# Both passages around an attention stage reordered: the next stage's first steps issued in the stage before

## The chip, the cores and the metric

The kernel runs on one core of a Trainium2 chip as one program. The metric is device time in microseconds, the median of several runs. The engines, as the profile names them: PE is TensorE's matmul (PEld its weight load), DVE is VectorE, ACT is ScalarE, POOL is GpSimd, and SP is SyncE, which issues the DMAs. Each engine runs its own queue in order, and they wait for each other by semaphores.

## The reference

One transformer layer of "macaron" form on x of shape (8, 512, 128), in fp32: half an FFN, attention, half an FFN.

```python
x = x + 0.5 * ffn(layernorm(x))
x = x + attn(layernorm(x))
x = x + 0.5 * ffn(layernorm(x))

# ffn: 8 experts of hidden size 176, all computed, the two best weighted
scores = softmax(xf @ w_router.T)
expert_weights, expert_indices = top_k(scores, 2)
h = silu(xf @ w1[e]) * (xf @ w3[e]);  y = h @ w2[e]
out = sum over the two chosen experts of weight * y

# attn: 16 heads of complex dimension 64, causal, distance-decayed
q, k, v = x @ Wq, x @ Wk, x @ Wv          # complex
qr, kr = q * phase, k * phase             # rotation by position
E = exp(clip(-mu * |t - t'|, -30, 0))
s = Re(qr . conj(kr));  V = a * (1 - E*E) + b
maha = max(|q|^2 + E*E*|k|^2 - 2*E*s, 0) / V
logits = coef * log1p(maha / nu) - 32 * log(V);  A = softmax(causal logits)
y = concat(Re(A v), Im(A v)) @ Wo
```

## The kernel before

`program` calls three stages one after the other: `dense_phase(0)`, `attention_phase`, `dense_phase(1)`. Each is a Block of its own: all engines finish a stage before any begins the next. Matmuls in the FFN and the projections are split in three (`mm3`, lines 71 to 73: high x low, low x high, high x high), so each operand exists as a high and a low part; ScalarE makes the high part by a copy and VectorE or GpSimd the low part by a subtraction.

**The FFN.** Tokens come in 8 batches of 512, a hidden layer of 8 x 176 units in 11 chunks of 128; a slot `e` (0 to 87) is one chunk of one batch. In a slot TensorE makes `products(e + 2)` (6 matmuls of 512 columns) and `down(e - 1)` (3), ScalarE `do_silu` (L406) and the high part of hid (L511), VectorE `gate` (L714, silu times up) and `weigh` (L722, times the router's weight), GpSimd the low part `hid_lo` (L593). Layernorm, transposition and routing of later batches are put in by tables of slots (`TURN_AT`, `ROUTE_AT`, `SPREAD_AT` and so on). Layernorm's inverse root is `root` on ScalarE (L416, L418: Ln, then Exp of -0.5 times it) and a Newton step `refine` on VectorE (seven small instructions, L631 to L637). ScalarE evaluates a function only with its table loaded; the loads are placed by the compiler, or by hand with `preload_act_table_set` (L475, L1235). The routing chain on VectorE is `route_gap` to `route_weights` (L665 to L709), some 19 small instructions, each waiting for the one before; `spread` (L299) transposes the expanded weights.

In the first FFN the finished batches are normalised again for attention during later slots (`AGAIN_AT`); the last two, 6 and 7, only after the last slot, by `root(5, 6, B)`, `normalise(B + 6)`, `normalise(B + 7)` and the transpositions of `turn_x`.

**Attention.** There are 128 pairs (16 heads by 8 batches), pair `n` of head `h = n // 8`. The stage is a software pipeline written out in full: in step `r` each engine runs `a_step`, which handles pair `r` and its neighbours. TensorE: `scores(r)` (L1065), `norms(r + 1)` (L1076, L1078), `project(r + 2)`, `turn(r - 1)` (L1101), `values` in the steps of even heads, `weigh(r - 2)` (L1124). VectorE: `peaks(r - 1)` (L1310), `distances(r)` (L1319, L1323), `query_norms(r + 1)`, `accumulate(r - 3)` (L1342), for the last head also `moments(r - 3)` (L1350, L1354, layernorm statistics for the second FFN), `turn_parts(r + 2)` (L1361, L1363: the projections times sine and cosine), `inverse(r - 1)`. ScalarE: `soften(r - 1)` (L1169), `key_norms(r + 1)`, `clamp(r)` (L1186), `turned_out(r - 1)` (L1193), `logs(r)` (L1199), `square(r + 2)` (L1205), `values_out`. GpSimd: `rotate(r + 1)` (L1254, "rot") and `spread(r + 1)` (L1262, "ek"). SP sends by_sin to the other half of the partitions (`crossed`) and loads each head's weights and tables (`load`). The per-head tables (decay, lam) come from `build...` functions, ahead of the steps for head 0. The steps begin at -2 (`FIRST`).

**The second FFN** begins with its serial head: variance and root of all batches, refine, normalise 0 and 1, four transpositions each, high and low parts, router products (L284, L286), products(0) and (1), routing, spread(0); then gate(0).

## Time and profile before

| | us |
|---|---|
| median of 3 runs | 1766.41 (1765.48 to 1767.93) |
| profiled execution | 1766.49 |
| its span (first to last instruction) | 1764.7 |

| engine | busy us | share of span |
|---|---|---|
| PE | 1665.2 | 94% |
| ACT | 1489.9 | 84% |
| DVE | 1473.1 | 83% |
| POOL | 986.2 | 56% |

The busy times are of the whole span. The page's strip of 40 slices shows where they are not met: TensorE's digits are 5 in slice 1, 7 and 6 in slices 6 and 7, and 7 in slice 35; these are the kernel's opening, the passage from first FFN to attention and the passage from attention to the second FFN. "Idle before" in a row of a timeline is how long that engine had stood still, with the instruction that released it.

### The profile page before, as it was taken

Reading aid. Unit: us, or ns where it says so; the run is one execution under the profiler, and the core shown is the slowest. Engines: PE = TensorE matmul, PEld = TensorE weight load, DVE = VectorE, ACT = ScalarE, POOL = GpSimd, SP = SyncE. Lnnn points to the kernel's source line nnn. Section 1 sums busy time; section 2 is a strip of 40 time slices with the busy share of each in tenths; the row PEclk is TensorE's granted clock in tenths of the full one; section 3 lists DMA queues with packets and bytes.
Section 4 is the critical chain, followed back from the end, with each engine's and each line's share of the span. In section 5 each row is a group of like instructions: output and inputs, shape, how many; then the busy total and the mean of one; then the engine's idle time right before and its main releaser. Section 6 shows DMA issues by size and latency. Waiting matters only on the chain. (4 is left out here: it accounts for less than half of the span.)

```text
span 1764.7 us, 30614 instructions
## 1 busy us (share of the span) xinstructions
PE 1665.2 (94%) x9664; PEld 1343.5 (76%) x9664; DVE 1473.1 (83%) x3330; ACT 1489.9 (84%) x2943; POOL 986.2 (56%) x841
## 2 busy tenths in 40 slices
PE   5999976999999999999999999999999999799998
PEld 4787854787887887788778778877877887577876
DVE  6777865899889988988998899899889889867675
ACT  5777765989999999999999999999989999666765
POOL 3554544566556656665665566566556656235565
PEclk9999987999999999999999999999999999989999
DMA  6000012222323232222223222222222222000000
GB/s 169 1 1 1 1 72 57 69 64 61 76 49 75 49 76 64 61 69 55 70 54 71 68 61 66 58 67 58 68 71 61 64 59 50 25 1 13 13 7 19
DMA packets 42978, 92.29 MB, mean 52 GB/s; under 512 B 7361, under 2 KB 19265, under 8 KB 42817
## 3 DMA queue, kind: packets, MB, share of 16 engines
q1 hardware_dynamic: 42816, 90.33, 20.5%
q8 instruction: 78, 1.28, 0.3%
q14 instruction: 84, 0.68, 0.1%
HBM read 17.95 MB, written 5.24 MB: 13 GB/s over the span
## 5 line engine op out<-in xcount | busy, mean ns | idle before, releaser
L1254 POOL TENSOR_TENSOR rot<-by_cos,crossed 128x1024 f32<-128x1024 f32 x128 | 305.1, 2383 | 485.8 <-PE pS L1065 244.2
L1262 POOL TENSOR_TENSOR ek<-decay,knorm 128x128 f32<-128x128 f32 (+3 forms) x512 | 432.3, 879 | 10.6 <-ACT knorm L1177 10.6
L593 POOL TENSOR_TENSOR hid_lo_d<-hid_d,hid_hi_d 128x512 fp32r<-128x512 f32 x176 | 230.8, 1311 | 238.4 <-ACT hid_hi_d L511 231.8
L1186 ACT ACTIVATE u<-u,qnorm 128x128 f32<-128x128 f32 (+3 forms) x512 | 246.3, 554 | 64.4 <-DVE u L1323 64.4
L1065 PE MATMUL pS<-rot 128*128 128x128 f32 (+3 forms) x1024 | 297.8, 434 | 0.1
L1169 ACT ACTIVATE z<-z,nmax 128x128 f32<-128x128 f32 (+3 forms) x512 | 281.1, 560 | 9.1 <-DVE nmax L1310 8.5
L1319 DVE SCALAR_TENSOR_TENSOR pS<-pS,ek 128x1280 f32<-128x1280 f32 x128 | 191.8, 1498 | 107.7 <-PE pS L1065 107.3
L1310 DVE CUSTOM_DVE_ANT_0 z<-u,lam,hp 128x128 f32<-128x128 f32 (+3 forms) x512 | 257.2, 555 | 11.8 <-ACT u L1199 10.3
L1065 PEld LDWEIGHTS pS<-rot 128*128 128x128 f32 x1024 | 165.1, 191 | 95.6 <-issue 61.5
L1323 DVE TENSOR_TENSOR u<-pS,decay 128x512 f32<-128x512 f32 (+1 forms) x256 | 199.0, 819 | 4.4
L1199 ACT ACTIVATE u<-u,hp 128x512 f32<-128x512 f32 (+1 forms) x256 | 196.4, 817 | 0.0
L1078 PEld LDWEIGHTS pV<-ones,squares 128*128 128x128 f32 x1024 | 135.3, 193 | 61.8 <-issue 61.8
L1101 PE MATMUL pS<-ident,z 128*128 128x128 f32 x1280 | 164.0, 274 | 7.7 <-DVE u L1323 4.1
L1101 PEld LDWEIGHTS pS<-ident,z 128*128 128x128 f32 x1280 | 147.3, 141 | 29.5 <-issue 5.1
L1124 PE MATMUL p<-val_odd,probT 128*128 128x128 f32 x1280 | 156.5, 278 | 8.2 <-issue 5.9
L511 ACT ACTIVATE hid_hi_d<-hid_d 128x512 fp32r<-128x512 f32 x176 | 111.1, 631 | 60.8 <-DVE hid_d L722 41.2
L1193 ACT ACTIVATE probT<-pS 128x1280 f32<-128x1280 f32 x128 | 158.6, 1239 | 4.1 <-PE pS L1101 1.9
L1124 PEld LDWEIGHTS p<-val_odd,probT 128*128 128x128 f32 x1280 | 148.7, 193 | 15.2 <-issue 15.2
L1361 DVE TENSOR_TENSOR by_sin<-pQK,sin 128x1024 f32<-128x1024 f32 x128 | 154.9, 1210 | 4.5 <-PE pQK L73 4.5
L1124 PE MATMUL p<-val_even,probT 128*128 128x128 f32 x1280 | 154.3, 276 | 2.4 <-issue 1.2
L1363 DVE TENSOR_TENSOR by_cos<-pQK,cos 128x1024 f32<-128x1024 f32 x128 | 155.1, 1212 | 0.0
L1076 PE MATMUL pV<-squares,ones 128*128 128x512 f32 x256 | 135.0, 609 | 18.8 <-ACT squares L1205 11.5
(239 smaller groups left out, 3570.6 us busy)
## 6 DMA issues: line engine op xcount, KB each, us to landing
crossed<-by_sin SPq DMA_DIRECT2D x256, 256.0 KB, 3.7
cos<-trig_d SPq DMA_DIRECT2D x64, 64.0 KB, 2.0
sin<-trig_d SPq DMA_DIRECT2D x64, 64.0 KB, 2.0
raw_d<-in_w SPq DMA_DIRECT2D x3, 704.0 KB, 8.9
x_sb<-in_x SPq DMA_DIRECT2D x4, 512.0 KB, 8.5
wqk_raw<-in_wqk SPq DMA_DIRECT2D x16, 128.0 KB, 3.6
out_x<-x_sb SPq DMA_DIRECT2D x8, 256.0 KB, 2.3
trig_d<-cos_t_d SPq DMA_DIRECT2D x1, 1024.0 KB, 4.4
```

What stands on the lines that cost most here:

```text
L593: g.tensor_tensor(hid_lo[:, par], hid[:, par], hid_hi[:, par].bitcast(F32), ALU.subtract).then_inc(lo_done, 1)
L1065: last = pe.matmul(s.pS[:, span(I)], rot[:, I * P:(I + 1) * P], rot[:, N:N + (I + 1) * P], start=True, stop=True)
L1101: last = pe.transpose(s.pS[:, col:col + P], z[:, col:col + P], s.ident[:])
L1124: last = pe.matmul(s.p7[:, I * P:(I + 1) * P], turned[:, OFF[I] + J * P:OFF[I] + (J + 1) * P], val[:, J * P:(J + 1) * P], start=(J == 0), ...
L1169: last = a.activation(z[:, span(I)], z[:, span(I)], ACT.Exp, bias=nmax[:, I:I + 1], scale=-1.0, accum_out=rsum[:, r % 4, I:I + 1])
L1186: last = a.activation(u[:, span(I)], u[:, span(I)], ACT.Relu, bias=qnorm[:, r % 2, I:I + 1])
L1199: a.activation(u[:, half], u[:, half], ACT.Ln, bias=hp[par][:, U_MIN:U_MIN + 1]).then_inc(S["ln_done"], 1)
L1254: g.tensor_tensor(rot[:], by_cos[:], crossed[:], ALU.add).then_inc(S["rot_done"], 1)
L1262: last = g.tensor_tensor(ek[:, span(I)], decay[par][:, span(I)], knorm[:, 0:(I + 1) * P], ALU.mult)
L1310: last = v.tensor_tensor_reduce(z[:, span(I)], u[:, span(I)], lam[par][:, near(I)], hp[par][:, NEG_COEF:NEG_COEF + 1], HIGHEST, ALU.add, A ...
L1319: v.scalar_tensor_tensor(s.pS[:, 0:SW], s.pS[:, 0:SW], -2.0, ek[:], ALU.mult, ALU.add).then_inc(S["w_done"], 1)
L1323: v.tensor_tensor(u[:, half], s.pS[:, half], decay[par][:, half], ALU.mult).then_inc(S["t_done"], 1)
```

## The change

Storage: several attention buffers and those of the second FFN's head become parts of one tile `early` (it also holds the first FFN's raw weights and trig tables), so that one stage can write what the next one uses; their semaphores (`s.S`, `s.D1`) are made once for all stages.

First FFN: head 0's weights (`wqk0`), tables and decay are prepared in slots 77 to 85; the projections of pairs 0 and 1, their sine and cosine products, the square and the norms of pair 0 are issued at its end, the first ahead of the last two `down`. The layernorm of batches 6 and 7 moves into attention's steps -1 to 1 (`late_...`). `FIRST` becomes -1. Every `root` is preceded by a preload of the table set that holds Ln and Exp.

Attention's last steps: the head of the second FFN (batches 0 and 1: variance, refine, normalise, transposition, router products, routing, products(0) and (1), silu(0), spread(0)) is spread over steps 124 to 129. The second FFN begins with gate(0); roots and refines of its later batches move to slots 1, 10, 14 and 19. In it the banks of g and u are swapped.

```diff
@@ dense_phase, SyncE @@
                 sp.wait_ge(trig_out, 48)
+                sp.wait_ge(wp_lo, 4)
+                sp.dma_start(s.wqk_raw, s.wqk[0]).then_inc(s.S["w_in"], 16)
+                for q, table in enumerate((1, 2, 2, 1)):
+                    rows = slice(q * DH // 2, (q + 1) * DH // 2)
+                    sp.dma_start(s.cos0[rows, :], s.trig_d[0, 0]).then_inc(s.S["trig_in0"], 16)
+                    sp.dma_start(s.sin0[rows, :], s.trig_d[table, 0]).then_inc(s.S["trig_in0"], 16)
+                sp.wait_ge(s.S["bs_done"], 1)
+                sp.dma_start(s.crossed[0:DH, :], s.by_sin[DH:P, :]).then_inc(s.S["crossed_in"], 16)
+                sp.dma_start(s.crossed[DH:P, :], s.by_sin[0:DH, :]).then_inc(s.S["crossed_in"], 16)
@@ dense_phase, TensorE @@
-                if first and b in REFINED:
+                if b in REFINED and (first or b < 3):
                     pe.wait_ge(rstd_done, REFINED[b])
...
                 if e + 2 < SLOTS:
                     products(e + 2)
+                if first and e == SLOTS - 1:
+                    pe.wait_ge(gated_done, SLOTS)
+                    pe.wait_ge(s.S["w_hi"], 1)
+                    pe.wait_ge(s.S["w_lo"], 1)
+                    first_projection(0)
                 if e > 0:
                     down(e - 1)
...
             down(SLOTS - 1)
             turn_y(B - 1)
             if first:
-                pe.wait_ge(hid_done, SLOTS)
-                turn_x(B + 6, w_bank[0])
-                turn_x(B + 7, w_bank[1])
+                pe.wait_ge(s.S["sq_done"], 1)
+                pe.wait_ge(s.S["cos_done"], 1)
+                first_projection(1)
+                pe.matmul(s.p6[:], s.ones[:], s.squares[:, N:2 * N], start=True, stop=True).then_inc(s.S["kn_done"], 1)
+                for I in range(TILES):
+                    last = pe.matmul(s.p5[:, I:I + 1], s.squares[:, I * P:(I + 1) * P], s.ones[:, 0:1],
+                                     start=True, stop=True)
+                last.then_inc(s.S["q2_done"], 1)
@@ dense_phase, ScalarE @@
             def root(n, b0, b1):
+                nc.scalar.preload_act_table_set("natural_log_exp_and_others")
                 a.wait_ge(var_done, n + 1)
...
                 if e in EXP_AT:
-                    if first:
+                    if first or e == EXP_AT[1]:
                         root(EXP_AT.index(e) + 1, *((5, B), (0, 3))[EXP_AT.index(e) - 1])
...
+                if first and e == 83:
+                    a.wait_ge(s.S["w_in"], 16)
+                    a.activation(s.wqk0[0], s.wqk_raw, ACT.Copy).then_inc(s.S["w_hi"], 1)
...
+            if first:
+                nc.scalar.preload_act_table_set("natural_log_exp_and_others")
+                a.wait_ge(s.S["arg_done"], 1)
+                a.activation(s.decay0, s.decay0, ACT.Exp).then_inc(s.S["decay_done"], 1)
+                a.wait_ge(s.S["cos_done"], 1)
+                a.activation(s.squares, s.pQK[:], ACT.Square).then_inc(s.S["sq_done"], 1)
             copy_out(B - 1)
-            if first:
-                root(5, 6, B)
-                a.wait_ge(rstd_done, 6)
-                normalise(B + 6, 0, TILES)
-                normalise(B + 7, 0, TILES)
-                high(B + 6, w_bank[0])
-                high(B + 7, w_bank[1])
@@ dense_phase, VectorE @@
                 if not first:
+                    if e == 1:
+                        refine(1, 2, 5, w_bank[1])
+                    if e == 10:
+                        variance(5, B)
+                    if e == 19:
+                        refine(2, 5, B, w_bank[0])
                     continue
...
+                v.wait_ge(s.S["trig_in0"], 128)
+                v.wait_ge(s.S["qk_done"], 1)
+                tt(two(s.by_sin), two(s.pQK[:]), both(s.sin0), ALU.mult).then_inc(s.S["bs_done"], 1)
+                tt(two(s.by_cos), two(s.pQK[:]), both(s.cos0), ALU.mult).then_inc(s.S["cos_done"], 1)
             add_out(B - 1)
@@ attention_phase, TensorE @@
                 if live(i, r):
                     scores(i, r)
-                if live(i, r + 1):
+                if n == PAIRS - 1:
+                    head_turn(0)
+                    head_turn(1)
+                if live(i, r + 1) and (i, r) != (0, -1):
                     norms(i, r + 1)
-                if live(i, r + 2):
+                if live(i, r + 2) and (i, r) != (0, -1):
                     project(i, r + 2)
-                if live(i, r - 1):
+                if i == 0 and r in (0, 1):
+                    turn_x(r)
+                if live(i, r - 1) and n != PAIRS:
                     turn(i, r - 1)
                 if live(i, r) and parity(r) == 0:
                     values(i, r)
                 if live(i, r - 2):
                     weigh(i, r - 2)
+                if n == PAIRS - 1:
+                    head_route(0)
+                    head_route(1)
+                if n == PAIRS:
+                    head_products(s.pQK)
+                    turn(i, r - 1)
+                if n == PAIRS + 1:
+                    head_spread()
+                    head_products_next(s.pS)
@@ attention_phase, ScalarE @@
                 if live(i, r - 1):
                     soften(i, r - 1)
+                if n == PAIRS - 3:
+                    head_root(0, 0, 2)
+                if n == PAIRS:
+                    a.wait_ge(D["gap_done"], 1)
+                    a.activation(s.e_s1[:, pair], s.gap1[:, pair], ACT.Exp).then_inc(D["exp_done"], 1)
+                    head_root(1, 2, 5)
                 if live(i, r + 1):
                     key_norms(i, r + 1)
+                if n == PAIRS - 1:
+                    head_high(0)
+                    head_high(1)
+                if i == 0 and r == -1:
+                    build(LN, 0, 0)
+                if i == 0 and r == 0:
+                    late_normalise(0)
+                    late_normalise(1)
                 if live(i, r):
                     clamp(i, r)
...
                 if live(i, r):
                     logs(i, r)
+                if i == 0 and r in (0, 1):
+                    late_high(r)
...
+                if i == 0 and r == -1:
+                    late_root()
+                if n == PAIRS:
+                    nc.scalar.preload_act_table_set("silu_and_others")
+                    a.wait_ge(D["guw_done"], 1)
+                    a.activation(s.silu1[:, 0], s.pQK[:, 0:N], ACT.Silu).then_inc(D["silu_done"], 1)
@@ attention_phase, VectorE: a_step @@
+                if i == 0 and r == 0:
+                    late_refine()
+                if n == PAIRS:
+                    accumulate(i, r - 3)
                 if live(i, r - 1):
                     peaks(i, r - 1)
                 if live(i, r):
                     distances(i, r)
+                if n == PAIRS - 1:
+                    head_low(0)
+                    head_low(1)
...
+                if n == PAIRS:
+                    head_gap()
+                    head_first()
...
+                if i == 0 and r == -1:
+                    late_moments()
+                if i == 0 and r == 0:
+                    build_back(0, 0)
+                if i == 0 and r in (0, 1):
+                    late_low(r)
+                if n == PAIRS - 4:
+                    head_variance(0, 2)
+                if n == PAIRS - 3:
+                    head_refine()
+                if n == PAIRS - 2:
+                    head_normalise()
+                if n == PAIRS - 1:
+                    head_variance(2, 5)
+                if n == PAIRS + 1:
+                    head_second()
+                    head_weights()
```

The `late_` and `head_` functions issue what their namesakes in the FFN issue (`late_high`: a copy of a 128x512 bank; `late_low`: the subtraction; `late_normalise`: four activations; `head_normalise`: eight VectorE instructions; `head_gap`, `head_first`, `head_second`, `head_weights`: the routing chain in four parts), on the buffers of `early`.

## Rows read from the trace of the kernel before

**Rows 1.** Stage windows: busy us (instructions) of PE, PEld, DVE, ACT, POOL; PE clock; DMA.

```profile
256.00:292.00 36.00, 16.27 (x48) 10.48 (x48) 11.55 (x29) 14.48 (x24) 8.22 (x8) 0.67 0.13 35
292.00:1522.00 1230.00, 1203.43 (x7569) 976.65 (x7570) 1105.04 (x2489) 1150.52 (x2341) 739.05 (x650) 1.00 0.26 63
1522.00:1559.00 37.00, 22.98 (x121) 19.68 (x120) 23.81 (x98) 17.29 (x36) 0.00 (x0) 0.73 0.00 1
...
1522.50:1542.60 20.10, 11.26 (x81) 10.48 (x80) 14.48 (x61) 9.24 (x20) 0.00 (x0) 0.90 0.00 0
```

**Rows 2.** Timeline, TensorE, first FFN: start, us, engine, line, tiles; in brackets idle before.

```profile
41.18 0.47 PE L71 MATMUL pS<-xT_hi,w_lo 128*128 128x512 f32 x1 [2.61 <-ACT silu_d L406]
...
74.37 0.50 PE L71 MATMUL pS<-xT_hi,w_lo 128*128 128x512 f32 x1 [1.31 <-ACT silu_d L406]
```

**Rows 3.** Timeline, ScalarE, table loads at a root, and at the second FFN's opening.

```profile
218.28 1.28 ACT L416 ACT_TABLE_LOAD   x1
...
219.80 1.28 ACT L418 ACT_TABLE_LOAD   x1
...
221.33 1.28 ACT L406 ACT_TABLE_LOAD   x1
...
1542.84 1.28 ACT L475 ACT_TABLE_LOAD   x1 [7.44 <-PEq L953]
1544.13 0.23 ACT L416 ACTIVATE root_y_d<-var_d 128x32 f32<-128x32 f32 x1
1544.39 0.23 ACT L418 ACTIVATE root_y_d<-root_y_d 128x32 f32<-128x32 f32 x1
```

**Rows 4.** Timeline, TensorE, passage from first FFN to attention.

```profile
258.46 0.40 PE L73 MATMUL p<-hid_hi_d,w_hi 128*128 128x512 f32 x1
...
276.20 0.76 PE L71 MATMUL pQK<-xT_hi,wqk_lo 128*128 128x512 f32 x1 [4.90 <-DVE wqk_lo L1290]
...
278.47 0.63 PE L73 MATMUL pQK<-xT_hi,wqk_hi 128*128 128x512 f32 x1
283.08 2.08 PE L1076 MATMUL pV<-squares,ones 128*128 128x512 f32 x2 [3.99 <-ACT squares L1205]
284.95 1.71 PE L1078 MATMUL pV<-ones,squares 128*128 128x1 f32 x8
```

**Rows 5.** Timeline, VectorE, passage and first steps of attention.

```profile
280.76 1.21 DVE L1363 TENSOR_TENSOR by_cos<-pQK,cos 128x1024 f32<-128x1024 f32 x1
...
291.73 1.49 DVE L1319 SCALAR_TENSOR_TENSOR pS<-pS,ek 128x1280 f32<-128x1280 f32 x1
...
310.47 1.50 DVE L1319 SCALAR_TENSOR_TENSOR pS<-pS,ek 128x1280 f32<-128x1280 f32 x1
```

**Rows 6.** Timeline, GpSimd, first pair of attention.

```profile
285.37 2.35 POOL L1254 TENSOR_TENSOR rot<-by_cos,crossed 128x1024 f32<-128x1024 f32 x1 [6.05 <-DMA crossed<-by_sin]
287.68 3.36 POOL L1262 TENSOR_TENSOR ek<-decay,knorm 128x128 f32<-128x128 f32 x4
```

**Rows 7.** Timeline, ScalarE, normalisation of pairs 6 and 7.

```profile
265.69 3.18 ACT L428 ACTIVATE xn_d<-x_sb,shift_d,rstd_d 128x128 f32<-128x128 f32 x8 [1.47 <-DVE shift_d L637]
```

**Rows 8.** Timeline, VectorE, passage from attention to second FFN.

```profile
1522.56 1.50 DVE L1319 SCALAR_TENSOR_TENSOR pS<-pS,ek 128x1280 f32<-128x1280 f32 x1 [0.32 <-PE pS L1065]
...
1546.26 1.11 DVE L643 TENSOR_SCALAR xn_d<-x_sb,mv,rstd_d 128x128 f32<-128x128 f32 x4
...
1553.33 0.22 DVE L665 COPY second_d<-pS 128x64 f32<-128x64 f32 x1 [2.81 <-PE pS L286]
...
1558.51 0.68 DVE L714 TENSOR_TENSOR gated_d<-pS,silu_d 128x512 f32<-128x512 f32 x1
```

**Rows 9.** Instructions of line 1319: ns min/median/max, first and last start.

```profile
L1319 DVE SCALAR_TENSOR_TENSOR pS<-pS,ek x128: 1486/1499/1500, 291.7 to 1522.6; 128x1280 f32<-128x1280 f32 x128
```

**Rows 10.** Timeline, TensorE, spread of batch 2 in both FFNs.

```profile
85.28 0.63 PE L299 MATMUL pV<-ident,wexp_d 128*128 128x128 f32 x4 [1.22 <-DVE shift_d L637]
...
1607.07 0.66 PE L299 MATMUL pV<-ident,wexp_d 128*128 128x128 f32 x4 [0.39 <-ACT wexp_d L447]
```

More of the change, by code:

```diff
@@ L145, in dense_phase @@
             half_pi = sb("half_pi", [P, 1])
-            angle, cos_t, sin_t, nsin_t = (sb(n, [P, 4, N]) for n in ("angle", "cos_t", "sin_t", "nsin_t"))
+            angle, cos_t, sin_t, nsin_t = (
+                s.early[:, 3 * HC * P + k * 4 * N:3 * HC * P + (k + 1) * 4 * N].rearrange("p (g t) -> p g t", g=4)
+                for k in range(4))
             head_sem, wr_in, ident_in, w13_in, w2_in, angle_in, cst_in, wvo_in = (sem(n) for n in (
@@ L336, in turn_y, with first_projection @@
                 last.then_inc(y_turned, 1)
+            def first_projection(b):
+                toks = slice(b * N, (b + 1) * N)
+                pe.wait_ge(xlo_done, B + b + 1)
+                for j in range(2):
+                    last = mm3(pe, s.pQK[:, j * N:(j + 1) * N], tuple(h[:, j * P:(j + 1) * P] for h in s.wqk0),
+                               (s.xT[0][:, toks], s.xT[1][:, toks]), True, True)
+                last.then_inc(s.S["qk_done"], 1)
             def value_turn(g):
@@ L1053, in a_step @@
                     load(i, building(FRONT, i, r))
-            load(0, 0)
             steps(nc.sync, a_step)
@@ L1113, in values, with turn_x, head_turn @@
                 last.then_inc(S["v_done"], 1)
+            def turn_x(j):
+                pe.wait_ge(S["late_xn"], j + 1)
+                wait(pe, S["late_lo"], j)
+                for q in range(TILES):
+                    last = pe.transpose(s.p7[:, q * P:(q + 1) * P], late_xn[j][:, q * P:(q + 1) * P], s.ident[:])
+                last.then_inc(S["late_xt"], 1)
+            def head_turn(j):
+                pe.wait_ge(D["xn_dve"], j + 1)
+                pe.wait_ge(S["sq_done"], PAIRS)
+                pe.wait_ge(S["cos_done"], PAIRS)
+                for q in range(TILES):
+                    last = pe.transpose(head_x[j][:, q * P:(q + 1) * P], s.xn1[:, j, q], s.ident[:])
+                last.then_inc(D["xt_done"], 1)
@@ new lines, in head_route @@
+            def head_route(b):
+                pe.wait_ge(D["xlo_done"], b + 1)
+                pe.wait_ge(S["norm_done"], PAIRS)
+                for q in range(TILES):
+                    t = b * TILES + q
+                    toks = slice(t * P, (t + 1) * P)
+                    pe.matmul(both_logits[:, t].rearrange("p a e -> p (a e)"), s.xT[0][:, toks], s.wr[:],
+                              start=True, stop=False)
+                    last = pe.matmul(both_logits[:, t, 0], s.xT[1][:, toks], s.wr[:, 0:NE], start=False, stop=True)
+                last.then_inc(D["logit_done"], 1)
@@ L1115, in weigh, with head_spread @@
+            def head_spread():
+                pe.wait_ge(D["wexp_dve"], 1)
+                for q in range(TILES):
+                    last = pe.transpose(s.p5[:, q * P:(q + 1) * P],
+                                        s.wexp1[:, 0, q].rearrange("p e j -> p (e j)"), s.ident[:])
+                last.then_inc(D["wb_done"], 1)
             def weigh(i, r):
                 n = i * 16 + r
+                if n == 0:
+                    pe.wait_ge(S["late_lo"], 2)
                 wait(pe, S["trc_done"], n + 1)
@@ L1363, in turn_parts, with late_moments @@
                 v.tensor_tensor(two(by_cos[:]), two(s.pQK[:]), both(cos[par]), ALU.mult).then_inc(S["cos_done"], 1)
-            def a_step(i, r):
+            def late_moments():
+                for I in range(TILES):
+                    last = v.bn_stats(stats[:, I, :], s.x_sb[:, 7 * TILES + I, :])
+                last.then_inc(S["late_stat"], 1)
+                v.wait_ge(S["late_stat"], 1)
+                for I in range(TILES):
+                    last = v.bn_aggr(s.mv[:, 7 * TILES + I, :], stats[:, I, :])
+                last.then_inc(S["late_mv"], 1)
+                v.wait_ge(S["late_mv"], 1)
+                v.tensor_scalar(s.late_var, s.mv[:, LATE, 1], LN_EPS, None, ALU.add).then_inc(S["late_var"], 1)
```

339 lines of the change are left out of this document (248 added, 91 removed).

## Prediction

> **What bounds the kernel now.** I read the stage windows first, then the timelines of both passages engine by engine, then every place where TensorE stands still in the FFN stages. In the stage windows [rows 1] the reader should compare TensorE's busy time with the length: attention has 1203.43 of 1230 us and ScalarE 1150.52, with the clock at 1.00, so nothing can be gained there except by fewer instructions, and the change takes none away. The two passages are different: 16.27 of 36 us between first FFN and attention (clock 0.67), 22.98 of 37 between attention and second FFN (0.73). There a chain of short dependent steps sets the time. A third place is inside the first FFN: TensorE stops for 2.61 and 1.31 us behind ScalarE's silu [rows 2], two stalls of each size (the other pair at 223 and 156 us), each where the layernorm's `root` runs. All sums are on the profiled execution, 1766.49 us with a span of 1764.7; that is 0.08 above the median, so I take them as equal.
>
> **Part 1, table loads in the first FFN.** One `root` costs ScalarE three loads: 218.28, 219.80, 221.33, 1.28 us each (for Ln, for Exp, back to silu) [rows 3]. The change puts one preload of a common set ahead. The second FFN's opening shows what that does: one load at 1542.84, then Ln at 1544.13 and Exp at 1544.39 with no load between [rows 3]. So each `root` loses one load. There are four within slots of the first FFN (at slots 2, 14, 47, 72), and TensorE and VectorE both wait behind each, for at least 1.30 us, so 4 x 1.28 = 5.1 us. Least: 0 if the other queues (VectorE's routing work behind them) take it back; and -5.1 if the preload is added and both loads stay. I take 5.1.
> The Trainium skill (ScalarE: Activation LUTs, What ACT_TABLE_LOAD costs) charges 1.28 us for the load and another 1.38 of draining for every switch. By it the four would give about 10.6 instead of 5.1. The trace disagrees with the drain: the Ln starts 0.01 us after its load ends [rows 3].
>
> **Part 2, first FFN to attention.** Before: the last down product starts at 258.46, then y is turned and added, layernorm of pairs 6 and 7 runs as a serial chain, the block ends, wqk comes from memory, and the first projection starts at 276.20 [rows 4]; the first `distances` at 291.73, that of pair 2 at 310.47 [rows 5].
> After, in times of the old trace (part 1 not yet taken off): the wqk, table and decay work of head 0 goes into slots 77 to 85, where TensorE is the bound, at no cost; its DMAs are issued after the trig table's write lands, 20 us early enough. The first projection stands ahead of the last two down products. These wait for GpSimd's hid_lo anyway, so its 1.4 us at full clock (half of 276.20 to 279.10 [rows 4]) costs nothing and it ends at about 257.0. VectorE's by_sin and by_cos (1.21 each [rows 5]) end at 259.4. ScalarE meanwhile loads a table and makes decay, squares the projections (about 1.0) to 260.5, and only then does `copy_out(7)` run, to 261.0: 1.5 us later than before, because the square was put ahead of it. TensorE turns y by 261.7, then the second projection and the norms. Norms are 2.08 + 1.71 at half clock [rows 4]. All at full clock: 1.4 + 1.9, end at 265.1; falling to half soon after 262: 267.7. With the block's end the attention starts (T0) at 265.4 to 268.0; I take 266.7, the middle, since the same engine idles for two stretches of 2 us just before.
> From T0: GpSimd's rot 2.35 and ek 3.36 [rows 6] make 5.7, but VectorE has by_sin, by_cos (which waits for rot), the late moments (8 instructions, about 1.6), ScalarE's late root (0.5) and seven refine steps (1.4) ahead of `distances(0)`: T0 + 7.2. The moved layernorm is not gone. The eight ScalarE normalisations, 3.18 us [rows 7], stand ahead of `clamp(0)`, and `late_high` stands after `logs` in steps 0 and 1 with VectorE's `late_low` (like the 0.68 of a 128x512 VectorE instruction [rows 8]) ahead of `peaks`. So `peaks` waits for the whole of logs, a copy and a subtraction. Stepping through the queues I get `distances(1)` at T0 + 18.8 and `distances(2)` at T0 + 29.8 (before, the three stood 18.7 us apart in all; now 22.6). That is 296.5 against 310.47: gain 14.0. Bounds: 18.7 if nothing of the late work shows (291.73 - 266.7 - 5.7 = 19.3, less 0.6 of waits), 9 if every late instruction adds on ScalarE and VectorE both. From there on the pace is the old one, 9.69 us a pair ((1522.6 - 291.7) / 127 [rows 9]).
>
> **Part 3, attention to second FFN.** Before: `distances` of the last pair at 1522.56, first gate of the FFN at 1558.51 [rows 8]. In between the tail's own VectorE work is 14.48 us [rows 1]; the rest is the serial head: layernorm, two normalise groups of four (1.11 each [rows 8]), turning, 16 router products, 19 small selection steps and the expansion, 1553.33 to 1558.51, 5.2 us [rows 8].
> After: variance, refine and eight normalisations (0.2 + 1.45 + 2.2) go into steps 124 to 126 of VectorE, which hardly idles there; 0.9 is hidden where `peaks` waited for ScalarE, so the last `distances` comes 2.95 later, at 1525.5. Then VectorE has the 14.5 of before, two `low` (1.4), a variance (0.2) and the 5.2 of routing: 21.3, and I add 2.2 for its waits on TensorE (the last weigh, router products behind a weigh) and ScalarE. End at 1549.0, with the block's end the first gate at 1549.6. TensorE's products(0), (1) are done by then, as they were before. Gain 8.9. The silu table and silu(0) lie under the weigh of the last pair.
> Some comes back in the second FFN: `refine(2)` at slot 19 now stands ahead of a spread that waits for it. The first FFN has that arrangement already, and TensorE stood still 1.22 there against 0.39 in the second [rows 10]: 0.8. Root at slot 14 puts two more activations (0.23 each as in [rows 3]) ahead of a silu on which VectorE waits: 0.45. `refine(1)` at slot 1, 1.4 on VectorE, has the lead of the products as cover: 0.2. Net 8.9 - 1.5 = 7.4. Bounds: 3 if the new waits of TensorE and VectorE on each other in steps 127 to 129 cost 4.4 more; 10 if the clock stays at 1.00 there.
>
> **Sum.** 5.1 + 14.0 + 7.4 = 26.5; 1766.5 - 26.5 = 1740.0. With the bounds: 0 + 9 + 3 = 12 gives 1754; 5.1 + 18.7 + 10 = 33.8 gives 1733.
>
> **Rivals.** (a) *The late work is dearer*: every addition in VectorE's and ScalarE's queues is paid in full, in both passages; 9 + 3 + 5.1 = 17: 1749. For it: attention has no free engine [rows 1]. Against: in the first steps all engines stand idle for part of the time. (b) *Passages shorter still*: clock stays at 1.00 through both and late work hides: 1733. For: TensorE has more to do in them than before; against: the waits of 2 us remain. (c) *The preload adds*: both loads of each `root` remain, part 1 turns into +5.1: 1750. Against: the opening of the second FFN [rows 3]. (d) *The loads also drain*, as the skill's page has it. As a mechanism of this kernel: each switch holds ScalarE's next instruction beyond the load, so one less gives more than 1.28. The stalls of 2.61 and 1.31 that can go [rows 2] bound it: twice 2.61 and twice 1.31, 7.8 instead of 5.1: 1737. The rows show no gap behind a load, so it has little chance. (e) *Slower*: attention's pace changes. It starts with GpSimd on rot and ek ahead of lam and with another phase between GpSimd, TensorE and VectorE; if this order locks in, `distances` waits for ek at every pair. From 26.5 / 128 = 0.21 us a pair the gain is gone; at 0.35, 45 us, the kernel takes 1785. For: rot is waited for by scores, and 9.69 us is above any one engine's work. Against: GpSimd is busy 739 of 1230 us [rows 1], so it catches up within a pair. (f) *It doesn't overlap*: TensorE's queue is in order, and the router products behind a weigh or the projection ahead of the down products could hold up what they precede by what they save; both passages then give nothing, part 1 stays: 1761.
>
> **How the numbers follow.** Forecast (1736 to 1744) 0.52; (a) 0.20, (b) 0.10, (c) 0.03, (d) 0.03, (e) 0.05, (f) 0.03, and 0.04 for anything between. The kernel's measurement can tell about 0.2%, 3.5 us, so faster means below 1762.9: all but (e), part of (f) and a bit: 0.93; within 0.2%: 0.02; slower 0.05. The range from 1732 to 1750 holds the forecast, (b), (c), (d) and most of (a), and leaves (e), (f) and the dear end of (a) out.
>
> **What would show it.** Part 1: two loads instead of three at each `root`, and stalls of 1.3 and 0.0 in place of 2.61 and 1.31. Part 2: first projection ending before the last two down products; TensorE idle about 2 us before the last turn of y; `distances` of pair 0 about 7 us after the block's end, pair 2 about 30 after it, and 19 us before the old time (parts 1 and 2 together). Part 3: the last `distances` 16 us ahead of the old time (19 less 3 of moved work); the first gate 28 ahead; a stall of TensorE of about 1.2 at slot 20. Wrong would be: a pace of other than 9.7 us a pair, three loads at a `root`, VectorE idle for over 4 us between the last `distances` and the first gate, or `distances(2)` under 25 or over 34 us after the start of attention.

## The result and the profile after

The changed kernel takes **1739.2 us** (median of 4 runs, 1735.46 to 1739.5) against 1766.07 for the kernel before on the same chip: ratio 0.9841, 95% interval [0.9824, 0.9858]. The forecast was 1740.0, range 1732 to 1750. In the profiled execution (1739.04 us) the span is 1737.3 us against 1764.7, 27.4 us less. The lines below answer to those of before; the line numbers are the new kernel's.

Stage windows of the changed kernel (columns as in [rows 1]). Attention keeps its density (1182.17 busy of 1210; before 1203.43 of 1230). In the window of the first passage TensorE is now busy for 26.22 of 36 us (before 16.27), and in the last passage it is VectorE that hardly rests: 36.23 of 40.

```profile
256.00:292.00 36.00, 26.22 (x119) 18.29 (x120) 24.98 (x53) 24.37 (x50) 18.61 (x17) 0.91 0.27 68
290.00:1500.00 1210.00, 1182.17 (x7451) 960.13 (x7450) 1086.19 (x2453) 1130.03 (x2306) 723.85 (x636) 1.00 0.25 63
1500.00:1540.00 40.00, 32.66 (x197) 27.27 (x198) 36.23 (x135) 25.04 (x52) 9.06 (x10) 0.96 0.01 1
```

Timeline of TensorE, the stalls behind a root in the first FFN, and batch 2's spread in the second. The first answers to 41.18 [2.61] of [rows 2]; no row answers to 74.37 [1.31], that stall is gone; the last answers to 1607.07 [0.39] of [rows 10] and is longer.

```profile
39.93 0.47 PE L71 MATMUL pS<-xT_hi,w_lo 128*128 128x512 f32 x1 [1.33 <-ACT silu_d L442]
...
219.65 0.50 PE L71 MATMUL pS<-xT_hi,w_lo 128*128 128x512 f32 x1 [1.31 <-ACT silu_d L442]
...
1579.66 0.63 PE L317 MATMUL pV<-ident,early 128*128 128x128 f32 x4 [1.24 <-DVE early L671]
```

Timeline of ScalarE at the root of slot 72: two loads, where [rows 3] has three.

```profile
215.94 1.28 ACT L451 ACT_TABLE_LOAD   x1
217.24 0.21 ACT L453 ACTIVATE root_y_d<-var_d 128x12 f32<-128x12 f32 x1
217.48 0.21 ACT L455 ACTIVATE root_y_d<-root_y_d 128x12 f32<-128x12 f32 x1
217.71 1.28 ACT L442 ACT_TABLE_LOAD   x1
```

Timeline of TensorE in the first passage, to be held against [rows 4]: the first projection begins at 251.53, ahead of the last down product (254.87; before 258.46), and the next pair's at 257.67, 2.8 us behind it.

```profile
251.53 0.50 PE L71 MATMUL pQK<-xT_hi,wqk_lo 128*128 128x512 f32 x1 [0.51 <-DVE gated_d L748]
...
254.87 0.39 PE L73 MATMUL p<-hid_hi_d,w_hi 128*128 128x512 f32 x1
257.26 0.66 PE L353 MATMUL p<-ident,yT_d 128*128 128x128 f32 x4 [2.01 <-ACT yT_d L447]
257.67 0.48 PE L71 MATMUL pQK<-xT_hi,wqk_lo 128*128 128x512 f32 x1
```

Timeline of VectorE in attention's first steps. L1488 is `distances` (L1319 of before): pair 0 at 269.67, pair 1 at 282.31, pair 2 at 294.20, against 291.73 and 310.47 for pairs 0 and 2 in [rows 5]. L1479 is `peaks`, in four pieces; two pieces are far longer than their size asks for: the 128x128 one 2.42 us, the 128x256 one 2.57 (0.47 a pair earlier).

```profile
277.73 0.69 DVE L1565 TENSOR_TENSOR xT_lo<-p,xT_hi 128x512 fp32r<-128x512 f32 x1 [2.09 <-ACT xT_hi L1351]
278.34 2.42 DVE L1479 CUSTOM_DVE_ANT_0 early<-early 128x128 f32<-128x128 f32 x1
...
281.90 0.47 DVE L1479 CUSTOM_DVE_ANT_0 early<-early 128x256 f32<-128x256 f32 x1
...
282.31 1.49 DVE L1488 SCALAR_TENSOR_TENSOR pS<-pS,ek 128x1280 f32<-128x1280 f32 x1
...
291.70 2.57 DVE L1479 CUSTOM_DVE_ANT_0 early<-early 128x256 f32<-128x256 f32 x1
...
294.20 1.49 DVE L1488 SCALAR_TENSOR_TENSOR pS<-pS,ek 128x1280 f32<-128x1280 f32 x1
```

Timeline of GpSimd beside them. The first row is where attention starts: GpSimd begins at 262.95, ScalarE and VectorE at 262.9. The `rotate` adds of pairs 2 and 3 end at 278.26 + 2.35 = 280.61 and 291.23 + 2.76 = 293.99, and the two long pieces end at 280.76 and 294.27.

```profile
262.95 2.35 POOL L1422 TENSOR_TENSOR early<-early 128x1024 f32<-128x1024 f32 x1 [8.71 <-POOLq L105]
...
278.26 2.35 POOL L1422 TENSOR_TENSOR early<-early 128x1024 f32<-128x1024 f32 x1 [2.77 <-DMA early<-early]
...
291.23 2.76 POOL L1422 TENSOR_TENSOR early<-early 128x1024 f32<-128x1024 f32 x1 [3.43 <-DMA early<-early]
```

Timeline of VectorE in the second passage ([rows 8]): last `distances` 1507.86 (before 1522.56), first gate 1530.21 (before 1558.51). The distance between them fell from 35.95 to 22.35 us.

```profile
1507.86 1.50 DVE L1488 SCALAR_TENSOR_TENSOR pS<-pS,ek 128x1280 f32<-128x1280 f32 x1 [0.30 <-PE pS L1110]
...
1515.78 1.13 DVE L1511 SCALAR_TENSOR_TENSOR x_sb<-p,rinv,x_sb 128x128 f32<-128x128 f32 x4 [1.08 <-PE p L1228]
...
1530.21 0.69 DVE L748 TENSOR_TENSOR gated_d<-pQK,early 128x512 f32<-128x512 f32 x1 [0.32 <-PEq L999]
```

**Two levels of the same program.** The changed kernel was run 17 times in all, 1735.4 to 1740.2 us, median 1739.4. Part of the spread can be read in the clock behind the stall at slot 47. Windows of the changed kernel's first profile, and of a second execution of the same program (control 0 below, span 1735.6):

```profile
158.00:160.00 2.00, 1.54 (x5) 0.81 0.00 0
160.00:162.00 2.00, 1.68 (x7) 0.50 0.00 0
162.00:164.00 2.00, 2.00 (x7) 0.50 0.02 4
164.00:166.00 2.00, 2.00 (x7) 0.50 0.00 0
```

```profile
158.00:160.00 2.00, 1.46 (x5) 1.00 0.00 0
160.00:162.00 2.00, 1.00 (x8) 1.00 0.00 0
162.00:164.00 2.00, 2.00 (x10) 1.00 0.02 4
164.00:166.00 2.00, 2.00 (x10) 1.00 0.00 0
```

The clock column (third from the right) is at 0.50, the lower level, for 6 us in one and at 1.00 in the other. The gate of slot 54 comes at 168.72 and 167.04: 1.7 us for the same work, of the 4.8 us by which the 17 runs differ.

### The profile page after: what moved, and what is told of

Its sections match the earlier page's. It is cut to its first block and busy times, and to the rows that moved or that the text cites. A ratio compares the mean times of both kernels' runs of the same rounds, so it can differ in the third digit from the quotient of the medians.

```text
span 1737.3 us, 30639 instructions
## 1 busy us (share of the span) xinstructions
PE 1655.6 (95%) x9664; PEld 1335.2 (77%) x9664; DVE 1476.4 (85%) x3350; ACT 1478.4 (85%) x2937; POOL 986.6 (57%) x841
## 5 line engine op out<-in xcount | busy, mean ns | idle before, releaser
L1422 POOL TENSOR_TENSOR early<-early 128x1024 f32<-128x1024 f32 x128 | 305.6, 2388 | 487.3 <-PE pS L1110 248.9
L1110 PE MATMUL pS<-early 128*128 128x128 f32 (+3 forms) x1024 | 299.2, 435 | 2.9 <-POOL early L1422 2.8
L1305 ACT ACTIVATE early<-early,qnorm 128x128 f32<-128x128 f32 (+3 forms) x512 | 246.3, 554 | 64.6 <-DVE early L1492 64.6
L1288 ACT ACTIVATE early<-early,nmax 128x128 f32<-128x128 f32 (+3 forms) x512 | 281.2, 560 | 16.8 <-DVE nmax L1479 16.2
L1488 DVE SCALAR_TENSOR_TENSOR pS<-pS,ek 128x1280 f32<-128x1280 f32 x128 | 191.7, 1498 | 109.1 <-PE pS L1110 108.8
L1110 PEld LDWEIGHTS pS<-early 128*128 128x128 f32 x1024 | 165.6, 192 | 98.9 <-issue 62.4
L1430 POOL TENSOR_TENSOR ek<-early 128x128 f32<-128x128 f32 (+3 forms) x256 | 216.2, 878 | 14.5 <-ACT early L1296 14.5
L1430 POOL TENSOR_TENSOR ek<-decay,early 128x128 f32<-128x128 f32 (+3 forms) x256 | 215.2, 874 | 2.3 <-ACT early L1296 2.2
L1150 PE MATMUL pS<-ident,early 128*128 128x128 f32 x1280 | 164.4, 274 | 8.2 <-DVE early L1492 6.8
L1150 PEld LDWEIGHTS pS<-ident,early 128*128 128x128 f32 x1280 | 147.3, 141 | 30.3 <-ACT early L1288 5.7
L1228 PEld LDWEIGHTS p<-val_odd,probT 128*128 128x128 f32 x1280 | 148.7, 193 | 16.8 <-issue 13.6
L1228 PEld LDWEIGHTS p<-val_even,probT 128*128 128x128 f32 x1280 | 147.9, 192 | 5.8 <-issue 5.8
L1123 PE MATMUL pV<-early,ones 128*128 128x512 f32 x254 | 132.8, 604 | 16.5 <-ACT val_odd L1331 9.9
L1479 DVE CUSTOM_DVE_ANT_0 early<-early,lam,hp 128x128 f32<-128x128 f32 (+3 forms) x256 | 129.1, 558 | 5.3 <-ACT early L1318 4.8
L1479 DVE CUSTOM_DVE_ANT_0 early<-early 128x128 f32<-128x128 f32 (+3 forms) x256 | 129.4, 560 | 4.5 <-ACT early L1318 3.4
```

The costliest lines, as they stand in the source:

```text
L1110: last = pe.matmul(s.pS[:, span(I)], rot[:, I * P:(I + 1) * P], rot[:, N:N + (I + 1) * P], start=True, stop=True)
L1150: last = pe.transpose(s.pS[:, col:col + P], z[:, col:col + P], s.ident[:])
L1228: last = pe.matmul(s.p7[:, I * P:(I + 1) * P], turned[:, OFF[I] + J * P:OFF[I] + (J + 1) * P], val[:, J * P:(J + 1) * P], start=(J == 0), ...
L1288: last = a.activation(z[:, span(I)], z[:, span(I)], ACT.Exp, bias=nmax[:, I:I + 1], scale=-1.0, accum_out=rsum[:, r % 4, I:I + 1])
L1305: last = a.activation(u[:, span(I)], u[:, span(I)], ACT.Relu, bias=qnorm[:, r % 2, I:I + 1])
L1422: g.tensor_tensor(rot[:], by_cos[:], crossed[:], ALU.add).then_inc(S["rot_done"], 1)
```

## The experiments

The starts below are of VectorE, in each kernel's profiled execution: the gate of slot 87, first FFN; `distances` of pairs 0 and 2 (d0, d2) and of the last pair; the first gate of the second FFN; and the span.

| kernel | median us | gate 87 | d0 | d2 | last d | gate, FFN 2 | span |
|---|---|---|---|---|---|---|---|
| before | 1766.1 | 254.39 | 291.73 | 310.47 | 1522.56 | 1558.51 | 1764.7 |
| changed | 1739.2 | 250.80 | 269.67 | 294.20 | 1507.86 | 1530.21 | 1737.3 |
| control 0 | 1740.1 | 249.17 | 268.05 | 292.59 | 1506.09 | 1528.45 | 1735.6 |
| e1 preload only | 1761.2 | 247.90 | 283.91 | 302.65 | 1516.37 | 1551.75 | 1757.6 |
| e2 no preload | 1747.1 | 255.40 | 274.60 | 301.69 | 1514.89 | 1537.25 | 1745.6 |
| e3 head serial | 1748.6 | 249.16 | 266.76 | 293.96 | 1504.61 | 1540.61 | 1746.6 |
| control 1 | 1738.3 | 251.10 | 268.70 | 295.45 | 1508.57 | 1530.91 | 1738.0 |
| e5 low after peaks | 1736.1 | 249.16 | 268.01 | 289.15 | 1502.67 | 1525.02 | 1732.1 |
| e6 moments late | 1738.4 | 251.72 | 270.59 | 297.91 | 1512.28 | 1532.63 | 1740.6 |
| e7 rotate held | 1735.5 | 251.01 | 269.87 | 290.56 | 1504.31 | 1526.66 | 1733.7 |
| b1 | 1743.4 | 251.51 | 270.41 | 295.64 | 1511.51 | 1537.69 | 1745.7 |
| b2 | 1733.3 | 249.49 | 268.35 | 288.36 | 1502.34 | 1522.69 | 1730.7 |
| b3 (b2 again) | 1733.9 | 249.53 | 267.14 | 288.88 | 1503.83 | 1524.18 | 1732.1 |
| control 2 | 1738.6 | 249.01 | 266.24 | 290.70 | 1504.21 | 1526.57 | 1733.6 |

Controls are the changed kernel itself, each on the chip of its group.

**First group: what each part is worth.** Part 1 alone:

```
 def root(n, b0, b1):          # kernel before
+    if first:
+        nc.scalar.preload_act_table_set("natural_log_exp_and_others")
     a.wait_ge(var_done, n + 1)
```

> The kernel before with nothing changed but the preload of the table at the head of each of the four roots in the first FFN. My theory (each removed load is 1.28 us of a stall of TensorE, but the half-clock stretch behind the stall at slot 47 ends at its old place and takes 1.5 us back, as the changed kernel's trace shows): gates end 3.6 us ahead at the last down product, 1766 - 3.6 = 1762.5 us. Rival 1 (the loads are worth their whole 5.1 us when alone): 1761. Rival 2 (a load drains the engine as well): 1755.5. Rival 3 (the preload adds a load): 1771.

Measured: 1761.24, ratio 0.9969 [0.9957, 0.9981], 5.35 us faster. My own theory (1762.5) was too dear by 1.3; rival 1 (1761) has the size. The starts of gates on VectorE in the profiled executions show it root by root (the four roots lie in slots 2, 14, 47 and 72):

| gate of slot | 2 | 5 | 16 | 50 | 54 | 76 | 87 |
|---|---|---|---|---|---|---|---|
| before | 32.67 | 43.61 | 74.35 | 161.04 | 171.10 | 229.00 | 254.39 |
| e1 preload only | 32.69 | 42.35 | 71.80 | 157.24 | 166.92 | 223.58 | 247.90 |
| changed | 32.70 | 42.36 | 71.77 | 157.14 | 168.72 | 225.38 | 250.80 |
| control 0 | 32.77 | 42.44 | 71.90 | 157.34 | 167.04 | 223.73 | 249.17 |
| e2 no preload | 32.73 | 43.69 | 74.42 | 161.16 | 171.21 | 229.13 | 255.40 |

From before to e1 each root gives 1.2 to 1.3 us, one load, and no more: 5.1 in all. That leaves no room for the draining or an added load. Two more gains at slots 54 and 87, 0.4 and 1.1, are clock: behind two of the three-load stalls the kernel before falls to the lower level, between 162 and 168 and between 224 and 232 (mean 0.57 there), and e1 stays at 1.00. And the edit reaches further than the four roots. The root of batches 6 and 7, behind the last slot, loses a load as well (timeline of ScalarE in the kernel before, below: the one at 262.72), which brings `distances(0)` another 1.3 nearer: 36.01 us behind gate 87 instead of 37.34. In the changed kernel this root has moved into attention, so e1's 5.35 is not part 1 alone. The 5.1, the clock's 1.4 and this 1.3 make the 7.8 by which pair 2 is ahead in the table above; 1.6 of it is lost again before the last `distances`, where e1's clock is at 0.57 from 1510 to 1514.

```profile
262.49 0.21 ACT L416 ACTIVATE root_y_d<-var_d 128x8 f32<-128x8 f32 x1 [1.69 <-DVE var_d L621]
262.72 1.28 ACT L418 ACT_TABLE_LOAD   x1
264.01 0.21 ACT L418 ACTIVATE root_y_d<-root_y_d 128x8 f32<-128x8 f32 x1
```

Part 1 taken out of the changed kernel:

```
 def root(n, b0, b1):          # changed kernel
-    nc.scalar.preload_act_table_set("natural_log_exp_and_others")
```

> The changed kernel without the preload in the roots (one preload at the start of both FFNs, as before). If part 1 is worth the same inside the changed kernel: 1739.2 + 3.6 = 1742.8 us for the first FFN's four roots, plus up to 1.3 for the root at slot 14 of the second FFN if its third load shows, so 1743 to 1744. Rival (the cover inside the changed kernel differs, loads are hidden): 1739 to 1740.

Measured: 1747.06, 6.9 over control 0, more than either theory. The gates above show the same four steps of 1.2 to 1.3 us against control 0, 5.1 in all, and the second FFN has the fifth: gate to end 208.35 against 207.15, where the root at slot 14 now has three loads. That is 6.3 of the 6.9. The two spans are 10.0 apart; the rest there is clock, as far as the windows tell: 0.4 and 0.8 behind the three-load stalls, and 2.5 between pairs 0 and 2, where e2 is at 0.50 from 288 to 292 and control 0 at 1.00.

Second passage undone: the head of the second FFN back in its own phase.

```
-    if n == PAIRS - 4: head_variance(0, 2)     # and all other head_* calls in attention
+    else:                                       # second FFN's opening, as before
+        root(0, 0, B)
+    a.wait_ge(rstd_done, 1); normalise(0, ...); normalise(1, ...); ...
```

> The changed kernel with the second passage put back as it was: the head of the second FFN (variance, refine, normalise, routing, silu of slot 0) runs in that phase after attention's end, nothing of it in attention's last steps. My theory, by the split read from the two traces (3.6 + 12.7 for the first FFN and first passage, 11.1 for the second passage): 1739.2 + 11.1 = 1750.3 us, and last distances to first gate 36.0 us. Rival (the prediction's sizes 7.4 for the second passage and 19.1 for the rest): 1746.6. If the gains of the two passages were not independent: outside 1746 to 1752.

Measured: 1748.63 against 1740.12 for control 0, between my theory (1750.3) and the rival (1746.6): part 3 is worth 8.5 by the medians and 11.0 by the two spans. The trace splits it. The moved work begins behind the `distances` of pair 124; from there to those of pair 127 e3 takes 28.37 us (before 28.35) and control 0 30.87 (changed kernel 30.79), so it costs 2.5. Of this 1.5 is one step, from pair 125 to 126, with the clock at 1.00 in both. Most of the rest, 0.9, is the last step, in which every kernel with the moved work falls to a mean of 0.84 or less while e3 and the kernel before stay at 1.00; e1, without the moved work, fell there too, so how much of the 0.9 the work itself takes stays open. The way from there to the gate is 22.36 instead of 36.00, and 1.2 is given back after the gate (206.0 and 207.15 to the end): 13.6 - 2.5 - 1.2 = 9.9. The table's last `distances` (1506.09 against 1504.61) are only 1.5 apart because e3 was 1.0 behind already at pair 124, ahead of any edit: its clock is at 0.50 from 280 to 284, control 0's at 1.00. That 1.0 is the rest of the 11.0. The medians lie 2.5 nearer together than the spans; three of control 0's four runs were at 1740, its profiled one at 1737.4, so I put that down to the clock, which is argued and not shown. Between 8.5 and 10 the size stays open; the forecast's 7.4 is under both.

> The changed kernel again, as the measure for the others of this group on the same chip: 1739.2 us, ratio to before 0.9848.

**Second group: what the first steps and the tail cost.** `late_low` out of the way of `peaks`:

```
     if live(i, r - 1): peaks(i, r - 1)
+    if i == 0 and r in (1, 2): late_low(r - 1)
...
-    if i == 0 and r in (0, 1): late_low(r)
```

> The changed kernel with the two late_low instructions of VectorE (2.1 and 0.8 us of wait for ScalarE's late_high ahead of them) moved behind the next step's peaks. My theory (that wait and the GpSimd add that then stretches a peaks instruction by 2.1 us are what part 2 cost over the forecast): peaks(0) starts when ScalarE's first logs end, 1.8 us sooner, is over when GpSimd's add begins, and distances(1) comes 3.6 us sooner; 1740.1 - 3.5 = 1736.6 us (1735 to 1738). Rival (the steps after are paced by the chain norms, key_norms, ek, scores, and take it back): 1739.5 to 1740.5.

Measured: 1736.09 (four runs, one of them 1744.78), span 3.5 under control 0's, whose clock was alike in the first FFN. Pair 1 came 9.31 after pair 0, where control 0 has 12.63. The medians' difference within the group, 2.2, is smaller than the intervals (0.9836 [0.9814, 0.9858] against 0.9835 [0.9821, 0.9848]), so the time alone would not carry it; the trace does. Timeline of VectorE: all `peaks` pieces have their short times, and the last of them has begun before GpSimd's add starts at 276.74.

```profile
274.80 0.35 DVE L1479 CUSTOM_DVE_ANT_0 early<-early 128x128 f32<-128x128 f32 x1 [0.82 <-ACT early L1318]
...
276.31 0.48 DVE L1479 CUSTOM_DVE_ANT_0 early<-early 128x256 f32<-128x256 f32 x1
```

Moments of the last three batches late (slots 2, 4, 6 of the second FFN):

```
-    if isinstance(i, int) and (H - 1) * B <= i * 16 + r - 3 < PAIRS:
+    if isinstance(i, int) and (H - 1) * B <= i * 16 + r - 3 < PAIRS - 3:
```

> The changed kernel with the moments of the last three batches (3 x 1.26 us on VectorE) taken out of attention's last steps and put into slots 2, 4 and 6 of the second FFN. My theory (VectorE is what paces the second passage): two of them lie ahead of the weights of slot 0 and one ahead of the first gate, so the gate comes 2.5 to 3.8 us sooner, 1740.1 - 2.6 = 1737.5 us with about 1 given back in the FFN's first slots. Rival (TensorE's weigh, ScalarE's exp and the turned tile pace the passage): under 0.8 us, 1739.3 to 1740.1. Rival 2 (the first slots of the FFN have no room on VectorE): same time, the gain given back there.

Measured: 1738.36 against 1738.27: nothing by the medians, with single runs up to 1747.8. By the trace the last `distances` to the gate is 20.35 instead of 22.35, and 0.9 is given back (208.0 to the end, 207.1 in control 1): 1.1 net, under the 2.6 that I expected. VectorE was the bound for 2.0 of the 3.8 us taken out; then TensorE is. Timelines of TensorE and VectorE: the last weigh waits for ScalarE's turned tile, two blocks of products follow, and VectorE stands 1.02 and 0.97 us.

```profile
1527.99 2.50 PE L1238 MATMUL p<-val_odd,probT 128*128 128x128 f32 x20 [1.33 <-ACT probT L1322]
1530.33 0.60 PE L1223 MATMUL pV<-ident,early 128*128 128x128 f32 x4
1530.68 0.48 PE L71 MATMUL pS<-xT_hi,w_lo 128*128 128x512 f32 x1
```

```profile
1530.53 1.13 DVE L1521 SCALAR_TENSOR_TENSOR x_sb<-p,rinv,x_sb 128x128 f32<-128x128 f32 x4 [1.02 <-PE p L1238]
1532.63 0.69 DVE L748 TENSOR_TENSOR gated_d<-pQK,early 128x512 f32<-128x512 f32 x1 [0.97 <-PEq L1009]
```

GpSimd's add held until the pair before has its peaks:

```
 def rotate(i, r):
     ...
+    if n in (2, 3): g.wait_ge(S["zred_done"], 2 * (n - 1))
     g.tensor_tensor(rot[:], by_cos[:], crossed[:], ALU.add)
```

> The changed kernel with GpSimd's rotate of pairs 2 and 3 held until VectorE's peaks of the pair before is done; nothing else is moved. My theory (a peaks instruction that starts beside a GpSimd add waits for that add's end): no peaks instruction of the first two pairs takes over 0.8 us, distances(1) comes 2.1 us sooner, the add ends 1.5 to 2 us later; the time falls by 0 to 2, 1739 us. Rival (first use, code loading: the stretch is the instruction's own): one peaks instruction of each pair still takes 2.4 to 2.7 us, distances(1) comes no sooner, 1740 to 1742.

Measured: 1735.46 (ratio 0.9831 [0.9816, 0.9846]; four runs, one of them 1741.27), span 3.6 under the changed kernel's first profile, and both have the 0.50 stretch in the first FFN. I had expected 0 to 2. Timelines of VectorE and GpSimd: no piece is stretched, pair 1 comes 10.55 after pair 0 (12.64 without the hold), pair 2 10.14 after pair 1 (11.89), and the add starts at the end of the peaks. The rival, that the stretch is the instruction's own, falls with it. A wait was added, and by the trace the kernel became faster; the medians (1738.27 for control 1) point the same way inside their intervals.

```profile
278.54 0.34 DVE L1481 CUSTOM_DVE_ANT_0 early<-early 128x128 f32<-128x128 f32 x1
...
280.02 0.48 DVE L1481 CUSTOM_DVE_ANT_0 early<-early 128x256 f32<-128x256 f32 x1
...
280.42 1.49 DVE L1490 SCALAR_TENSOR_TENSOR pS<-pS,ek 128x1280 f32<-128x1280 f32 x1
```

```profile
280.68 2.39 POOL L1424 TENSOR_TENSOR early<-early 128x1024 f32<-128x1024 f32 x1 [4.98 <-DVE nmax L1481]
```

> The changed kernel once more, as the measure of this group on the same chip: 1740.1 us.

**Third group: together.** b1 has the edits of e7 and e6; b2 moves ScalarE's `late_normalise(1)` from ahead of `clamp(0)` to the end of its step as well; b3 is b2 once more.

> The changed kernel with GpSimd's rotate of pairs 2 and 3 held behind the peaks and the moments of the last three batches in the second FFN's slots. If the two gains add: distances(2) comes 3.7 to 6 us sooner after distances(0) than in the changed kernel (20.7 against 24.5 to 26.8), last distances to gate 20.4 instead of 22.35, with 0.8 of it given back in the slots: 1738.3 - 3.8 - 1.2 = 1733.3 us (1732 to 1735). Rival (the hold only moves the loss to a later pair): 1736.5 to 1738.

> The kernel of this group with both edits, and ScalarE's late_normalise(1) (1.6 us) moved from ahead of clamp(0) to the end of its step, where ScalarE waits 1.8 us for the peaks. My theory (in step 0 ScalarE paces the step): clamp(0) starts 1.0 us sooner and distances(1) with it: 1733.3 - 1.0 = 1732.3 us. Rival (turn_x(1) and late_high(1) come later and the wait moves to late_low(1)): 1733.3 or up to 1 more.

> The changed kernel once more, as the measure of this group on the same chip: 1739 us.

> The kernel with all three edits (rotate held behind the peaks, moments late, late_normalise(1) late) once more, to see whether its 1733.3 us was the kernel or the luck of TensorE's clock, since its neighbour without the third edit had 1741.9 to 1747.5 us in four of five runs at granted clocks of 0.985 to 0.989. If it is the kernel: 1732 to 1736 us again, clock 0.991 or more in every run. If it is luck: some of its runs too are at 1741 to 1748 us with clocks of 0.985 to 0.989.

Measured: b2 1733.3 (0.9813 [0.98, 0.9827]) and b3 1733.94 (0.9815 [0.9801, 0.9828]); nine runs from 1731.95 to 1736.31, against 1735.4 to 1740.2 for 17 of the changed kernel. It is the fastest version here, 5 us under the changed kernel, and b3's clocks (0.993 to 0.995) say that it is the kernel and not luck. The third edit brings pair 1 1.6 us nearer to pair 0 than e7 has it (8.99 against 10.55), and pair 2 0.7 nearer (20.01 against 20.69; 21.74 in b3, whose clock falls there); in the medians that can't be seen, they are at the rival's 1733.3 and not at 1732.3. b1 missed its expectation by 10: 1733.42, and four runs of 1741.85 to 1747.51 with clocks of 0.985 to 0.989. Windows of TensorE in b1, two stretches:

```profile
276.00:280.00 4.00, 1.61 (x5) 0.99 0.47 120
280.00:284.00 4.00, 3.38 (x10) 0.50 0.00 0
284.00:288.00 4.00, 4.00 (x13) 0.50 0.02 6
1514.00:1518.00 4.00, 2.46 (x15) 0.69 0.01 2
1518.00:1522.00 4.00, 4.00 (x21) 0.50 0.00 0
1522.00:1526.00 4.00, 4.00 (x19) 0.50 0.01 4
```

The clock falls to the lower level after TensorE stood still for 3.00 us (280.62, waiting for ScalarE's values), and again in the tail, where last `distances` to gate is 26.18 instead of 20.35: 5.8 us. In b2 the same wait is 1.37 us, and its windows there are at 1.00; in b3, the same program, the wait is 1.46 and the clock falls nevertheless (b2 first, then b3):

```profile
276.00:280.00 4.00, 3.17 (x16) 1.00 0.00 0
280.00:284.00 4.00, 3.14 (x27) 1.00 0.34 68
```

```profile
276.00:280.00 4.00, 3.34 (x14) 0.83 0.02 4
280.00:284.00 4.00, 4.00 (x26) 0.75 0.14 33
```

Over all traces of kernels with this passage: control 1, e2, e3, e6 and b1 fell behind waits of 2.99 to 3.01, e5 behind 2.81 and b3 behind 1.46; the changed kernel's first profile, controls 0 and 2 and e7 did not, behind waits of 2.85 to 2.93, nor did b2. So the length of that one wait doesn't settle it. That b1's edits raise the chance of a fall in the tail is suggested by four runs of five. Runs above the 1740.2 that the changed kernel never passed in 17 are also found in e5 (one of four), e6 (two of five) and e7 (one of four), but in none of the nine of b2 and b3, which have b1's two edits as well; what sets it stays open.

## Why the prediction was right, point by point

The total was right (26.5 forecast, 26.9 by the medians), with luck in it: the parts have errors of opposite sign.

| | forecast | medians | profiled spans |
|---|---|---|---|
| part 1 (e1, with the load behind the last slot) | 5.1 | 5.35 | 7.1 |
| part 2 (the rest) | 14.0 | 12.6 | 11.0 |
| part 3 (control 0 to e3) | 7.4 | 8.5 | 11.0 |
| sum (before to control 0) | 26.5 | 26.5 | 29.1 |

The clock differs between the profiled executions, so the spans carry up to 2 us of it for each part. The stretches compared below are chosen where it is the same, or the difference is named. One row of the changed kernel's VectorE is read in part 2, the instruction ahead of the gate of slot 87 (250.80):

```profile
249.07 1.21 DVE L983 TENSOR_TENSOR wqk_lo<-early,wqk_hi 128x256 fp32r<-128x256 f32 x1
```

- **Part 1**: mechanism and size right. Two loads at each root, stalls of 1.33 and none as forecast, and 1.2 to 1.3 us at each of the four roots in e1's and e2's gates. In the changed kernel's first profile only 3.6 of it was seen, which I took for its size; the gate of slot 76 in control 0 (5.3 ahead of before) and in e1 (5.4) shows that the difference is the 0.50 stretch at 160 to 166. The Trainium skill (ScalarE: Activation LUTs, What ACT_TABLE_LOAD costs) charges 1.38 us of draining besides; by that figure the four would have made an estimated 10.6. The steps of 1.2 to 1.3 and the Ln 0.02 us after its load speak against it here, and with it against rival (d).
- **Part 2**: right in kind, and some 1.5 too high, with three errors in it. One term was put at nothing: the preparation of head 0 in slots 77 to 85, "where TensorE is the bound, at no cost". From gate 76 to gate 87 e1 takes 24.32 us and the changed kernel 25.42 (25.40 to 25.45 in its controls), all at clock 1.00: 1.1 us. Of this 0.85 is in the last slot, where the gate stands behind VectorE's subtraction for wqk, the row above. The way to attention's start was right (8.0 from the last down product, forecast 8.2), and `distances(0)` 6.8 after it (7.2). The next step that failed is that of pairs 1 and 2: forecast 22.6 us from `distances(0)` to that of pair 2 (29.8 - 7.2), measured 24.5, in another run of the same kernel 26.8. The term missing is the GpSimd add that holds a `peaks` piece for 2.1 us in each of the two pairs: with the hold taken away e7 has 20.7. So without it the forecast would have been 1.9 too dear. That the late layernorm holds pair 1 up was foreseen, and e5 shows what taking its wait away gives. Third, the old pace doesn't begin at pair 2: to pair 3 it is 9.85 instead of 10.76, 0.9 gained. Together: from the last down product to pair 2 it is 39.3 us instead of 52.0, so 12.7 - 1.1 + 0.9 = 12.5.
- **Part 3**: mechanism right, and too low because of one size. The moved work costs 2.4 to 2.5 (forecast 2.95), a lower clock in the last step included. The way from the last `distances` to the gate was forecast as 21.3 of VectorE's work and 2.2 of waits with the block's end on top, 24.1; it is 22.35, with VectorE busy for 20.05 and in waits for 1.08 and 0.32, so both terms were too dear. VectorE as the pacing engine is borne out by e6, to 2.0 us. The clock stayed at 1.00 from 1505 on (the 0.96 of the window from 1500 comes from a fall before it), the condition of rival (b), whose bound of 10 for this part is met. The give-back was 0.9 to 1.2 (forecast 1.5), and the stall of 1.24 at batch 2's spread is where it was put.
- **The signs named beforehand**: the first gate is 28.3 ahead (28), pair 2 31.3 after attention's start (about 30). Pair 2 is 16.3 before the old time and not 19, and the last `distances` 14.7 and not 16: some 1.6 of each is the 0.50 stretch in the first FFN of this execution; in control 0, without it, they are 17.9 and 16.5.
- Rivals: (c) and (d) fall with e1's steps, (f) with e3 and with part 2's size; (e) too: from pair 8 to pair 125 the changed kernel takes 1131.29 us, before 1131.26. (a) put parts 2 and 3 at 9 and 3; both measured above. (b) holds for part 3 (10) and not for part 2 (18.7).

## What to carry to other kernels

Overlapping two phases moves their layernorms and copies into queues that were in step; follow each queue for some steps after the seam, since an engine that runs ahead can start where it holds another up, and a wait put in its way (e7) or a reordering (e5) may be worth more than the last microsecond of overlap. Before a gain of 1 to 3 us is read off two traces, look at the granted clock in both and repeat the kernel: here the same program differed by up to 5 us, and one part's size by 2.
